# dt products of odd channel blocks on the array's upper 64 rows, in a Mamba and ternary feed-forward layer

## The reference, cut to what matters

```python
x_dbl = jnp.einsum('bld,ed->ble', x, x_proj_w)     # 64 + 16 + 16 columns
dt = x_dbl[..., :dt_rank]
Bm = x_dbl[..., dt_rank:dt_rank + d_state]
Cm = x_dbl[..., dt_rank + d_state:]
dt = jax.nn.softplus(jnp.einsum('blr,dr->bld', dt, dt_proj_w) + dt_proj_b)
deltaA = jnp.exp(jnp.einsum('bld,dn->bldn', dt, A))
deltaB_u = jnp.einsum('bld,bln,bld->bldn', dt, Bm, x)
# h = deltaA_t * h + deltaB_u_t ; y_t = sum over n of h * C_t
```

## Time and profile before

| what | us |
|---|---|
| median of 3 runs | 4741.44 |
| lowest and highest run | 4734.76, 4742.01 |
| profiled execution, its own time | 4733.51 |
| its span, from first to last instruction | 4731.7 |

### The profile page before, as it was taken

The page is one execution under the profiler, slowest core; times in us unless marked ns, Lnnn a source line. Parts: engine busy times, 40 slices in busy tenths (PEclk is TensorE's granted clock), DMA queues, the critical chain, the costliest instruction groups (busy, mean ns, idle before and its releaser), DMA issues.

```text
span 4731.7 us, 85297 instructions
## 1 busy us (share of the span) xinstructions
PE 4423.0 (93%) x23362; PEld 3138.7 (66%) x23362; DVE 3941.4 (83%) x4785; ACT 3429.0 (72%) x6626; POOL 3162.0 (67%) x2462
## 2 busy tenths in 40 slices
PE   7999998999999898989898989899987899999998
PEld 4666666666666566656565666566655688888887
DVE  6999999999999898989898999899999644444444
ACT  5889898989898989888989888888987322222221
POOL 4797979898989888888888898989798200000000
PEclk8999999999999999999999999999999999999999
DMA  3333333333333333333333333333344100111101
GB/s 112 103 98 104 112 101 112 101 116 103 107 111 108 113 101 112 103 104 110 110 108 104 108 109 109 110 103 109 104 128 131 49 36 28 34 35 35 35 35 36
DMA packets 233417, 436.66 MB, mean 92 GB/s; under 512 B 24016, under 2 KB 24144, under 8 KB 232464
## 3 DMA queue, kind: packets, MB, share of 16 engines
q1 hardware_dynamic: 232976, 431.55, 29.1%
HBM read 397.38 MB, written 34.08 MB: 91 GB/s over the span
## 4 chain that ended last, share of the span: by engine, by line
POOL 33%; PE 27%; issue 19%; ACT 12%; DVE 8%; POOLq 1%; ACTq 0%; DVEq 0%; DMA 0%; SPq 0%
POOL dbu L649 26%; PE ht L1442 9%; PE y L1455 5%; PE gemm L1455 5%; DVE h L978 4%; ACT ch L717 4%; ACT decay L703 3%; PE gemm L1233 3%; PE ht L1285 2%; POOL x L586 2%; PE y L1290 2%; POOL carry L626 2%; POOL dtx L599 2%; POOLq L54 1%; POOL soft L591 1%
## 5 line engine op out<-in xcount | busy, mean ns | idle before, releaser
L978 DVE TENSOR_TENSOR_SCAN h<-decay,carry,dbu 128x512 f32<-128x512 f32 x2048 | 2526.5, 1269 | 189.2 <-ACT decay L703 124.9
L649 POOL TENSOR_TENSOR dbu<-dtx,bb 128x1024 f32<-128x1024 f32 x1024 | 2442.4, 2385 | 59.9 <-DVE dtx L1078 52.6
L703 ACT ACTIVATE decay<-dt,aneg 128x512 f32<-128x512 f32 x2048 | 1439.6, 705 | 264.7 <-DVE h L978 257.5
L1285 PE MATMUL ht<-ident,h 128*128 128x128 f32 x8192 | 1263.3, 284 | 256.9 <-ACT ch L717 178.4
L717 ACT ACTIVATE ch<-ht,ct 128x256 f32<-128x256 f32 x3328 | 1405.6, 484 | 123.6 <-PE ht L1285 123.1
L1285 PEld LDWEIGHTS ht<-ident,h 128*128 128x128 f32 x8192 | 970.6, 145 | 781.5 <-ACT ch L717 379.1
L1233 PE MATMUL gemm<-xt,win 128*128 128x512 f32 x1984 | 975.0, 600 | 17.0 <-ACT z L769 14.3
L1290 PEld LDWEIGHTS y<-ident,ch 128*128 128x128 f32 x6656 | 789.0, 144 | 243.8 <-issue 226.5
L1290 PE MATMUL y<-ident,ch 128*128 128x128 f32 x6656 | 894.0, 278 | 2.4 <-DVE x L1005 2.0
L898 ACT ACTIVATE hr<-ht,b1c 128x512 f32<-128x512 f32 x256 | 176.3, 689 | 753.0 <-PE ht L1442 753.0
L626 POOL TENSOR_TENSOR carry<-h,ones_pair 128x2 f32<-128x2 f32 x1022 | 289.9, 284 | 470.1 <-DVE h L978 454.3
(11 more groups left out here) (112 smaller groups left out, 3854.5 us busy)
## 6 DMA issues: line engine op xcount, KB each, us to landing
bb<-b_rows SPq DMA_DIRECT2D x1024, 256.0 KB, 3.5
win<-w_in SPq DMA_DIRECT2D x256, 256.0 KB, 2.7
xres<-x_tm SPq DMA_DIRECT2D x16, 1024.0 KB, 6.1
x<-xres SPq DMA_DIRECT2D x16, 1024.0 KB, 5.6
xr<-x SPq DMA_DIRECT2D x16, 1024.0 KB, 5.3
out<-xr SPq DMA_DIRECT2D x16, 1024.0 KB, 4.3
xt<-x_cm SPq DMA_DIRECT2D x15, 1024.0 KB, 6.5
raw<-w SPq DMA_DIRECT2D x8, 1024.0 KB, 7.4
```

The lines of the kernel that those rows point to most:

```text
L649: nc.gpsimd.tensor_tensor(dbu[:, u % 2, :, :], dtx[:, pair(q), :], bb[:, u % BB_RING:u % BB_RING + 1, :].to_broadcast([P, 2, TC]), ALU.mul ...
L703: nc.scalar.activation(DA[j][:, :], dt[:, c.par, i, :], ACT.Exp, scale=aneg[:, i, n:n + 1])\
L978: nc.vector.tensor_tensor_scan(h[:, H_SLOT[u], j, :], DA[j][:, :], dbu[:, u % 2, j, :], carry[:, c.par, n, i:i + 1], ALU.mult, ALU.add).th ...
L1285: ins = nc.tensor.transpose(HT[k][:, tb % 2, j * P:(j + 1) * P], h[:, H_SLOT[u], j, tb * P:(tb + 1) * P], ident[:, :])
```

## The change

Dt's weights get 128 partitions instead of 64, and the same 64x1024 matrix is loaded into both halves. The semaphore of the weights counts five loads. `take_xd` copies the first 64 rows of x's projection a second time, to partitions 64 to 127 of the unused second half of the buffer in which `xdbl` lies; this copy comes ahead of the old one. The dt product of an odd block takes its weights and its data from the upper 64 partitions, after a wait for that copy; those of even blocks stay as they are. Every product has the same operands' values as before.

```diff
--- before.py
+++ after.py
@@ -226,7 +226,7 @@
         win = sb("win", [P, 2, KM, P])
         wout = sb("wout", [P, NB, DM])
         wxp = sb("wxp", [P, NB, XD])
-        wdt = sb("wdt", [DTR, DI])
+        wdt = sb("wdt", [P, DI])
         ident = sb("ident", [P, P])
         cw = sb("cw", [P, NB, KC])
         cb = sb("cb", [P, NB])
@@ -262,6 +262,7 @@
         shift = sb("shift", [P, TB])
 
         xdbl = rounded[0:XD, 1, 0, :]
+        upper = rounded[DTR:2 * DTR, 1, 1, :]
 
         HALF = 4 * NB // 2 * TC
         homes = (("dt", 0), ("dt", HALF), ("soft", 0), ("rounded", 0), ("x", 0), ("x", HALF), ("xt", 0), ("dt", 2 * HALF))
@@ -317,6 +318,7 @@
         a_set = sem("a_set")
         full = {kind: sem(f"{kind}_full") for kind in KINDS}
         read = {kind: sem(f"{kind}_read") for kind in KINDS}
+        upper_ready = sem("upper_ready")
         state_zero = sem("state_zero")
         corr_step = sem("corr_step")
         corr_ready = sem("corr_ready")
@@ -379,7 +381,7 @@
         y_ready = sem("y_ready")
         stored = [sem("stored0"), sem("stored1")]
 
-        N_WEIGHTS = 4
+        N_WEIGHTS = 5
         SCANS = 2 * UNITS
         N_CH = 2 * len(BY_ACT)
         N_SUMS = len(BY_ACT)
@@ -502,7 +504,8 @@
             for dst, src in ((bdt, b_dt), (dsk, d_skip)):
                 sp.dma_start(dst[:, :], src).then_inc(weights_in, 16)
             sp.dma_start(wxp[:, :, :], w_xp.rearrange("(i p) e -> p i e", p=P)).then_inc(weights_in, 16)
-            sp.dma_start(wdt[:, :], w_dt).then_inc(weights_in, 16)
+            for half in range(2):
+                sp.dma_start(wdt[half * DTR:(half + 1) * DTR, :], w_dt).then_inc(weights_in, 16)
             for i in range(2, NB):
                 wait_full(sp, "x", first, i - 2)
                 load_win(i % 2, "x", i)
@@ -734,6 +737,7 @@
             def take_xd(f):
                 wait(act, dt_ready, f, NP, 0)
                 wait_full(act, "xd", f, 0)
+                nc.scalar.activation(upper, xd_bank(f)[0:DTR, :], ACT.Copy).then_inc(upper_ready, 1)
                 nc.scalar.activation(xdbl, xd_bank(f)[0:XD, :], ACT.Copy).then_inc(read["xd"], 1)
 
             def take_ct(f):
@@ -1257,8 +1261,11 @@
                 if i == 0:
                     wait_read(pe, "xd", f, 0)
                 room("dt", f, i)
-                nc.tensor.matmul(dt_bank(f, i)[:, :], wdt[:, i * P:(i + 1) * P], xdbl[0:DTR, :], start=True,
-                                 stop=True).then_inc(full["dt"], 1)
+                rows = slice(i % 2 * DTR, (i % 2 + 1) * DTR)
+                if i % 2:
+                    wait(pe, upper_ready, f, 1, 1)
+                nc.tensor.matmul(dt_bank(f, i)[:, :], wdt[rows, i * P:(i + 1) * P], upper if i % 2 else xdbl[0:DTR, :],
+                                 start=True, stop=True).then_inc(full["dt"], 1)
 
             def out_proj(p, tb, parts, room):
                 if 0 in parts:
```

## The result

The changed kernel is slower: 4766.77 us median of 20 runs against 4737.59 for 20 runs of the kernel before, a ratio of 1.0057 with a 95% interval of 1.005 to 1.0063, or 29 us. Forecast were 4747 us, 0.13% more. One thing must be known of these runs: they lie at two levels. Three of the 20 took 4746.7 to 4749.2 us, the other 17 took 4762 to 4772. The kernel before has one level, 4733 to 4742. The profiled execution of the changed kernel (4763.69 us, span 4761.8) is one of the upper level.

The account below looks back on a forecast made before the run. The prediction took the recurrence, with PE, DVE, ACT and POOL coupled, as the bound. Copies cost 5.6 us in the loop plus 0.5 in the prologue, other terms 0: about 6 us, 4747 us on the runs' scale, range 4736 to 4757.

Parts of the forecast that it names:

- What bounds the kernel, and the feed-forward part: Recurrence, 60 to 3430 us: coupled engines, PE and DVE each 94% busy; the 1191 us feed-forward part behind it stays unchanged.
- The copy, per chunk: New ACT copy in the loop: 0.5 us on ACT, 0.37 per chunk passed on, 5.6 us for 15, bounds 3.2 to 9.6.
- 0.5 us of delay just fits: ACT's decays in the loop: first done at 1588.7, its scan starts at 1589.30, so 0.5 us later does not delay it.
- 0.37 us per chunk: Chain through PE to DVE's second additions: dt product 0 starts 0.5 us later, less 0.13 slack, leaves 0.37 per chunk.
- slack of 0.13: At DVE's second additions: they start at 1594.23, scans end at 1594.10; the 0.13 us was subtracted from the copy's delay.
- The copy in the prologue: Ahead of the old copy at 41.62: costs 0.5 us, bounds 0 and 0.64; no gain entered for products side by side.
- The odd products in the loop: Odd dt products on the upper rows, 60 in the loop: cost change 0, bounds plus or minus 2.9 us.
- The added wait: PE's wait on upper_ready before each odd dt product: cost 0, upper bound 2.2 us, lower bound 0.
- The weights loaded twice: One more 256 KB load on SP's queue in the prologue: cost 0, at worst 0.6 us.
- The whole copy and a dearer product: Rival, PE chain: copy 0.64 plus product 1 dearer by 0.19, 0.83 per chunk, 13 us slower, 4754 us; chance 0.27.
- Absorbed: Rival: PE's slack and ACT's idle time take up the loop copy, only the prologue's 0.5 us stays, 4742 us; chance 0.18.
- Side by side: Rival: odd products run while neighbours do; 1.05 us less on PE, 0.68 per chunk net, faster, 4732 us; chance 0.12.

Follow-up runs that it names:

- b_copy_low: The kernel before plus a second copy of x's projection on ACT, written to partitions 0 to 63 and read by nobody; 4747.66 us, ratio 1.0017.
- a_late: The changed kernel with the upper copy behind the copy of z, product 0 waiting for the first copy alone, no upper_ready waits; 4740.27 against 4740.52 us, ratio 1.0.
- b_copy: The kernel before plus only the second copy on ACT to partitions 64 to 127, read by nobody; 4752.05 against 4741.81 us, ratio 1.0024.
- a_lower: The changed kernel with all dt products on the lower 64 rows, second copy, waits and second weight load kept; ratio 1.0056, executions at 4766.7 to 4769.3 us.
- b_waits: The kernel before plus one always satisfied PE wait ahead of each odd dt product, nothing else; run twice, ratios 1.0023 and 1.0029.

## Why the prediction was wrong, step by step

**What bounds the kernel, and the feed-forward part: right.** The stretch in which DVE, ACT and PE hand delays to each other was the right one, and the place of the copy too. From the last copy in the loop to the end it is 1323.4 us before and 1323.6 in the changed kernel.

**The copy, per chunk: right in mechanism, undersized.** The step that failed is "I take 0.5, nearer to the observed distance". On ACT it measured 0.87 us. The starts of three activations that write from partition 0 on were taken for one that writes from partition 64 on. With such a start the overlap with the activation ahead and the one behind is lost. The slack at the scans was then too small: "0.5 us of delay just fits" held for 0.47 (b_copy_low, 0.05 late), not for 0.87 (0.39 late). "0.37 us per chunk", the step by the chain through PE, measured 0.47 in b_copy_low and 0.80 in the changed kernel, with PE's first dt product late by 0.47 and 0.81: the delay went through in full. The "slack of 0.13" that was taken off was read the wrong way round. The additions started 0.13 after the scans ended because they waited for PE, so the slack was on DVE's side, as a_late shows (scans 0.20 later, additions not). 0.80 for 15 chunks are 12 us, against the 5.6 forecast and the upper bound of 9.6; b_copy measured 10.

**The copy in the prologue: wrong, and small.** Forecast were 0.5 us and no gain from products side by side.

```profile
41.17 0.59 ACT L740 ACTIVATE rounded<-decay 64x512 f32<-64x512 f32 x1 [1.35 <-PE decay L1247]
41.78 0.59 ACT L741 ACTIVATE rounded<-decay 96x512 f32<-96x512 f32 x1
...
42.52 1.13 PE L1267 MATMUL gemm<-rounded,wdt 64*128 64x512 f32 x4 [1.39 <-ACT rounded L741]
...
43.73 1.26 ACT L752 ACTIVATE dt<-gemm,bdt 128x512 f32<-128x512 f32 x2 [1.36 <-PE gemm L1267]
...
45.03 1.06 ACT L759 ACTIVATE soft<-dt 128x1024 f32<-128x1024 f32 x1
```

Products 0 and 1 take 1.13 us together, where the timeline of before has 1.95, and the two evacuations go at 1.26 us instead of the 1.46 of the earlier trace rows. ACT begins the absolute values at 45.03 and did so at 45.07 before. The gain pays for the copy.

**The odd products in the loop: right.** The new copy's row and the products' row of the changed kernel (ns min/median/max, first and last start):

```profile
L740 ACT ACTIVATE rounded<-gemm x15: 588/589/590, 220.2 to 3437.6; 64x512 f32<-64x512 f32 x15
```

```profile
L1267 PE MATMUL gemm<-rounded,wdt x248: 589/589/693, 42.5 to 3459.4; 64*128 64x512 f32 x124
```

A product's record has its old length, 589 ns, as the earlier trace rows had it, and a_lower has the time of the changed kernel. That first row also gives the interval between chunks, (3437.6 less 220.2) / 14, or 229.8 us against 227.6: 2.2 us more.

**The added wait: the step that failed most.** "Cost 0", with the "upper bound, if each shows, 0.037 times 60, 2.2 us", priced the execution of these instructions. It left out that they make PE's loop longer by 8 instructions. At the loop's place that brings the pair of fetches at each of the six branches, with a restart of PE 1.6 us later and, behind most, a lower clock: about 3 us each, 16 to 18 us in all. None of the rivals had this place. The bound from the row of one wait was no bound, since a row of durations says nothing of where a program's blocks lie.

**The weights loaded twice: nothing of it shows.** a_late has that load and stands at 1.0.

**The rivals.** "The whole copy and a dearer product" had the sign and named 4754 us, and the step of its copy was the better one, but its dearer product does not exist. Had the wait cost nothing, the three executions at 4747 to 4749 would have been the result: inside the range, and beside the forecast by luck, as the copy was undersized. "Absorbed" is what a_late shows, with the copy in another place. "Side by side" is shown for the array (1.13 us for two) and did not help in the loop.

## What to carry to other kernels

A wait that is always satisfied was not free in a hardware loop of some 5400 instructions: look at the idle time for "issue" behind the branch, and at the instruction queue there, before and after any edit that changes the number of instructions, and try the same edit with padding ahead of the loop before it is judged (8 instructions of it changed nothing here, 40 took the stall away). A copy that is needed late belongs behind those that are needed early, even on an idle engine, and with its own semaphore. Two levels among the executions of one kernel, as here, deserve a profile of each.

## What was not expected of the hardware

- PE behind a taken branch restarts 4.1 to 4.5 us after DVE's scans of that place began, or 5.6 to 6.0 where two 16 KB blocks of instructions start together; that costs about 1.6 us directly and, at five of the six branches, as much again by the clock (0.76 to 0.78 granted over 7 us; 1.00 at the fifth). With one and the same program (b_waits) it happened in 16 executions of 20 and not in four.
- An activation that writes from partition 64 on began only when the activation ahead had ended (1597.68 after 0.93 us from 1596.73), and the one behind it, which writes from partition 0 on in the same memory, only when it had ended (0.62 us after its start, its length being 0.59). Written from partition 0 on, starts are 0.48 us apart at a length of 0.64. The Trainium skill ("VectorE: DVE Perf Modes", Two Vector instructions with no wait between them) states for VectorE that an instruction whose output starts in another quadrant of 32 partitions than the last one into the same memory is held until all earlier ones have finished. The trace shows the like on ScalarE.
- Two products of 64 rows on different halves of the array, one behind the other in PE's queue, took 1.13 us together, where one alone took 1.12 and two on the same half 1.95.
